# Three target tiles side by side instead of two in the attention stage of a two-layer graph kernel

## What is computed

```python
h = maximum(layernorm(x), 0)
x = x + max over neighbours of h            # layer 0, one row of adj per node
h = maximum(layernorm(x), 0)
g = h @ W                                   # layer 1: graph attention
e = (g @ a1)[:, None] + (g @ a2)[None, :]
e = where(e > 0, e, 0.2 * e)
att = softmax(where(adj > 0, e, -9e15), axis=1)
x = x + elu(att @ g)
```

## Time and profile before

| | |
|---|---|
| median of 3 runs | 797.32 us |
| profiled execution | 796.32 us, span 793.9 us |
| TensorE busy (matmul) | 708.5 us, 89% |
| VectorE busy | 722.7 us, 91% |
| ScalarE busy | 486.0 us, 61% |
| GpSimd busy | 283.4 us, 36% |
| mean granted TensorE clock | 0.985 |

### The profile page before, as it was taken

How to read it: one execution, slowest core, us unless ns; L and a number is a source line. 1 busy time by engine, 2 the same in 40 slices (tenths; PEclk the granted TensorE clock), 3 DMA queues, 4 the chain that set the end, 5 groups by cost and what they waited for, 6 DMA issues and landing times.

```text
span 793.9 us, 14766 instructions
## 1 busy us (share of the span) xinstructions
PE 708.5 (89%) x5592; PEld 484.5 (61%) x5592; DVE 722.7 (91%) x1120; ACT 486.0 (61%) x615; POOL 283.4 (36%) x258
## 2 busy tenths in 40 slices
PE   1788999999999999999999999788899999999995
PEld 1344444444444444444444444477789999999995
DVE  8899889999999999999999999999888998898894
ACT  2978888888888888888888888363523010010000
POOL 0612033443443443443443443453513432132130
PEclk9999999999999999999999999889999999999998
DMA  9699777997787777777777762723425444344410
GB/s 305 243 365 362 264 250 217 272 332 218 239 258 215 244 255 216 245 251 218 248 249 217 250 214 80 265 60 102 133 68 192 156 171 160 128 165 159 142 45 16
DMA packets 62856, 162.55 MB, mean 205 GB/s; under 512 B 6400, under 2 KB 11136, under 8 KB 58688
## 3 DMA queue, kind: packets, MB, share of 16 engines
q1 hardware_dynamic: 53776, 138.75, 50.8%
q0 software_dynamic: 9008, 22.82, 11.8%
HBM read 117.51 MB, written 44.04 MB: 203 GB/s over the span
## 4 chain that ended last, share of the span: by engine, by line
PE 40%; ACT 23%; DVE 18%; issue 11%; DMA 5%; POOL 1%; ACTq 0%; DVEq 0%; SPq 0%
PE pick_ps L667 21%; ACT edge_t L367 11%; PE pick_ps L570 7%; DVE acc L825 7%; PE order_ps L551 7%; ACT depth L376 7%; ACT first L375 4%; DVE rest L1004 4%; DMA found<-subset_max,entry 3%; PE late_ps L583 2%; DVE rest L814 2%; PE late_ps L542 2%; DMA subset_max<-keys 2%; POOL h_lo L310 1%; DMA best<-x 1%
## 5 line engine op out<-in xcount | busy, mean ns | idle before, releaser
L825 DVE TENSOR_TENSOR acc<-pick_ps,acc 128x1024 f32<-128x1024 f32 x248 | 303.0, 1222 | 28.2 <-PE pick_ps L570 23.7
L339 POOL DMA_INDIRECT found<-subset_max,entry x192 | 205.6, 1071 | 297.2 <-DVE entry L837 198.5
L667 PE MATMUL pick_ps<-keys,rest 128*128 128x129 f32 x2048 | 237.5, 277 | 6.8 <-DVE rest L1004 6.7
L667 PEld LDWEIGHTS pick_ps<-keys,rest 128*128 128x128 f32 x2048 | 233.7, 193 | 13.1 <-DVE rest L1004 11.4
L1004 DVE SCALAR_TENSOR_TENSOR rest<-depth,curves_sb,stage 128x512 f32<-128x512 f32 x256 | 200.7, 814 | 21.1 <-ACT curves_sb L455 5.2
L375 ACT ACTIVATE first<-order_ps,neg 128x1024 f16<-128x1024 f32 x128 | 142.6, 1114 | 61.2 <-PE order_ps L551 61.2
L376 ACT ACTIVATE depth<-order_ps,mid 128x1024 f16<-128x1024 f32 x128 | 141.7, 1107 | 0.0
L367 ACT ACTIVATE edge_t<-late_ps 128x1024 f16<-128x1024 uint16 x128 | 131.1, 1024 | 2.8 <-PE late_ps L542 2.8
L551 PE MATMUL order_ps<-edge_t,order_w 128*128 128x512 f16 x256 | 79.5, 393 | 38.2 <-ACT edge_t L367 30.8
L570 PE MATMUL pick_ps<-first,h_hi 128*128 128x512 f16 x256 | 98.1, 383 | 6.9 <-DVE acc L825 6.8
L542 PEld LDWEIGHTS late_ps<-ident_h,stage 128*128 128x128 f16 x1024 | 69.6, 100 | 49.2 <-DMA stage<-adj 13.2
(11 more groups left out here) (135 smaller groups left out, 517.9 us busy)
## 6 DMA issues: line engine op xcount, KB each, us to landing
stage<-adj SPq DMA_DIRECT2D x64, 1024.0 KB, 5.4
edge_units<-edge_t SPq DMA_DIRECT2D x64, 512.0 KB, 4.5
stage<-edge_units SPq DMA_DIRECT2D x32, 1024.0 KB, 5.1
subset_max<-keys POOLq DMA_DIRECT2D x12, 512.0 KB, 8.6
found<-subset_max,entry POOLq DMA_INDIRECT x192, 4.3
best<-x SPq DMA_DIRECT2D x4, 512.0 KB, 6.2
subset_max<-x POOLq DMA_DIRECT2D x4, 512.0 KB, 8.7
out<-keys POOLq DMA_DIRECT2D x7, 256.0 KB, 3.3
```

Source lines behind the costliest of these rows:

```text
L339: nc.gpsimd.indirect_dma_start(found[:, n % NG, s, :], None, subset_max, bass.IndirectOffsetOnAxis(entry[:, n, s:s + 1], 0)).then_inc(gath ...
L667: last = nc.tensor.matmul(out_ps(q, b), weight[:, n % WEIGHTS, b * P:(b + 1) * P], wh[:, c, :], start=c == 0 and b % 2 == 0, stop=c == C - ...
L825: V.tensor_tensor(acc[:, q % 2, :], pick_ps[k][:, :], acc[:, q % 2, :], ALU.max).then_inc(raised, 1)
```

## The change

Tiles 0, 1 and 2 now walk the source groups side by side (`TRIO = 3`), over groups 0 and 1, 2 and 3, 4 and 5, 6, and 7: products 0 to 95. Then come tiles 3 to 7. The twelve accumulators lie three to a bank in banks 0 to 2 and the fourth blocks of all three tiles in bank 3; tile 3 uses banks 6 and 7, later tiles banks 0 to 3 in pairs as before. `limit` has four slots. `bound(2)` moves into the part of groups 2 and 3, behind move(3) and ahead of curve(2). Side work on VectorE and TensorE has new product numbers. The sums of the three tiles are copied out together when product 95 is done. The core of the diff:

```diff
+        TRIO = 3
+        ORDER = [(q, c) for lo, hi in ((0, 2), (2, 4), (4, 6), (6, LAST), (LAST, GR)) for q in range(TRIO) for c in range(lo * ROWS, hi * ROWS)]
+        ORDER += [(q, c) for q in range(TRIO, TILES) for c in range(C)]
...
+        THIRD = 136
+        trio_ps = lambda q, b: banks[q][:, b * THIRD:b * THIRD + D + 1] if b < TRIO else banks[TRIO][:, q * THIRD:q * THIRD + D + 1]
+        pair_ps = lambda q, b: banks[(6 if q == TRIO else q % 2 * 2) + b // 2][:, b % 2 * APART:b % 2 * APART + D + 1]
...
+        row_ps = lambda g: banks[(4, 5, 0, 1, 5, 4, 5, 5)[g]]
+        col_ps = lambda g: banks[(6, 6, 4, 5, 4, 5, 4, 4)[g]]
+        source_ps = lambda q: banks[2 if q < 2 else 4 + q % 2]
...
# ScalarE
                     normalise(i)
                     move(PARTS[i][1] - 1)
+                    if i == 2:
+                        bound(2)
                     for g in range(*PARTS[i]):
                         curve(g)
                         gather_wh(g)
-                bound(2)
-                norm(0)
-                norm(1)
-                for q in range(2, TILES):
+                bound(TRIO)
+                for q in range(TRIO):
+                    norm(q)
+                for q in range(TRIO, TILES):
...
# TensorE, behind mix(n)
-                    if n in (8, 9):
-                        columns(n - 6)
-                    if n == 9:
-                        project(2)
-                    if n in (10, 11, 14):
-                        rows((10, 11, 14).index(n) + 4)
-                    if n == 11:
-                        project(3)
-                    if n in (25, 26, 29):
-                        columns((25, 26, 29).index(n) + 4)
-                    if n in (27, 30, 33):
-                        project((27, 30, 33).index(n) + 4)
-                    if n == 40:
-                        rows(LAST)
-                    if n == 52:
-                        columns(LAST)
-                    if n == 54:
-                        project(LAST)
-                    if n == 56:
-                        sources(2)
+                    if n in (10, 11):
+                        columns(n - 8)
+                    if n == 12:
+                        sources(2)
+                    if n in (12, 14):
+                        project(n // 2 - 4)
+                    if n in (18, 20, 27):
+                        rows((18, 20, 27).index(n) + 4)
+                    if n in (40, 42, 46):
+                        columns((40, 42, 46).index(n) + 4)
+                    if n in (42, 46, 50):
+                        project((42, 46, 50).index(n) + 4)
+                    if n == 52:
+                        rows(LAST)
+                    if n == 75:
+                        columns(LAST)
+                    if n == 77:
+                        project(LAST)
+                    if n == 82:
+                        sources(TRIO)
...
# VectorE, ahead of weigh(n): product numbers before -> after
# add(2), add(3)            1, 2   -> 2, 3      stat(2), stat(3)        3, 4   -> 4, 5
# moments(2)                5      -> 6         fold(7)                 6      -> 18
# scales(2)                 7      -> 8         join(26), join(27)      9, 17  -> 13, 21
# search(29), name(29)      10     -> 11        merge and add 4, 5      13, 14 -> 24, 27
# stat(4), stat(5)          15, 16 -> 28, 29    merge(6), add(6)        18     -> 31
# stat(6), moments(3)       19     -> 33        scales(3)               22     -> 36
# search(30), name(30)      24     -> 26        search(31), name(31)    28     -> 40
# join(28), join(29)        27, 30 -> 44, 48    over                    32     -> 52
# join(30)                  40     -> 56        join(31), merge, add 7  47     -> 67
# stat(7), moments(4)       48     -> 69        scales(4)               50     -> 72
+                    if n - WEIGHTS + 1 == ENDS[TRIO - 1]:
+                        for k in range(TRIO):
+                            sums(k)
+                        for k in range(TRIO):
+                            invert(k)
+                    if n - WEIGHTS + 1 in ENDS[TRIO:]:
+                        sums(ENDS.index(n - WEIGHTS + 1))
                         invert(ENDS.index(n - WEIGHTS + 1))
```

More of the change, by code:

```diff
@@ L180, in layers @@
         weight = rest.rearrange("p s w -> p (s w)").bitcast(F32).rearrange("p (s t) -> p s t", t=TI)
[L181 removed]
+        limit = depth[:, :, :].rearrange("p s w -> p (s w)").bitcast(F32).rearrange("p (s t) -> p s t", t=TI)
         wide = keys.rearrange("p h r w -> p (h r w)")
@@ L667, in mix @@
                         last = nc.tensor.matmul(out_ps(q, b), weight[:, n % WEIGHTS, b * P:(b + 1) * P], wh[:, c, :],
-                                                start=c == 0 and b % 2 == 0, stop=c == C - 1 and b % 2 == 1)
+                                                start=c == 0 and starts(q, b), stop=c == C - 1 and stops(q, b))
                     last.then_inc(mixed, 1)
@@ L993, in cap @@
                     dve.wait_ge(limited, q + 1)
-                    V.tensor_scalar(limit[:, q % 2, :], limit[:, q % 2, :], STEEP, None, ALU.min).then_inc(capped, 1)
+                    V.tensor_scalar(limit[:, q % 4, :], limit[:, q % 4, :], STEEP, None, ALU.min).then_inc(capped, 1)
                     dve.wait_ge(capped, q + 1)
@@ L1003, in weigh, with sums @@
                         dve.wait_ge(mixed, n - WEIGHTS + 1)
-                    V.scalar_tensor_tensor(out=weight[:, n % WEIGHTS, :], in0=limit[:, q % 2, :], scalar=slope[:, c:c + 1],
+                    V.scalar_tensor_tensor(out=weight[:, n % WEIGHTS, :], in0=limit[:, q % 4, :], scalar=slope[:, c:c + 1],
                                            in1=units[:, m % EDGES, k * TI:(k + 1) * TI], op0=ALU.max, op1=ALU.mult).then_inc(made, 1)
-                def invert(q):
-                    dve.wait_ge(mixed, ENDS[q] + 1)
+                def sums(q):
+                    dve.wait_ge(mixed, ENDS[max(q, TRIO - 1)] + 1)
                     for b in range(ROWS):
@@ L1035, in _ @@
                         cap(q)
[L1036 to L1040, removed]
+                    if n in (2, 3):
+                        add(n)
+                    if n in (4, 5):
+                        stat(n - 2)
+                    if n == 6:
                         moments(2)
-                    if n == 6:
-                        fold(TILES - 1)
-                    if n == 7:
+                    if n == 8:
@@ L1045, in _ @@
                         scales(2)
-                    if n == 9:
-                        join(C - 6)
-                    if n == 10:
+                    if n == 11:
                         search(C - 3)
                         name(C - 3)
[L1051 to L1056, removed]
-                        join(C - 5)
@@ L1058, in _ @@
-                    if n == 18:
+                    if n == 13:
+                        join(C - 6)
+                    if n == 18:
+                        fold(TILES - 1)
+                    if n == 21:
+                        join(C - 5)
+                    if n in (24, 27):
+                        merge(n // 3 - 4)
+                        add(n // 3 - 4)
+                    if n == 26:
+                        search(C - 2)
+                        name(C - 2)
+                    if n in (28, 29):
+                        stat(n - 24)
@@ L1059, in _ @@
+                    if n == 31:
                         merge(6)
                         add(6)
-                    if n == 19:
+                    if n == 33:
                         stat(6)
                         moments(3)
-                    if n == 22:
+                    if n == 36:
                         scales(3)
[L1066 to L1070, removed]
@@ L1071, in _ @@
-                    if n == 28:
+                    if n == 40:
                         search(C - 1)
                         name(C - 1)
-                    if n == 30:
+                    if n == 44:
+                        join(C - 4)
+                    if n == 48:
                         join(C - 3)
-                    if n == 32:
+                    if n == 52:
                         dve.wait_ge(entry_ready, C)
```

49 lines of the change are left out of this document (25 added, 24 removed).

## The result

The changed kernel takes 794.02 us (median of 5 runs, 792.97 to 795.24) against 797.94 for the kernel before in the same rounds: ratio 0.9957, 95% interval 0.9938 to 0.9976. Measured again in other rounds it was 794.49 us, ratio 0.9965 (0.9951 to 0.9979). The forecast was 794.2 us. So it is faster, by about 0.4%. The profiled execution took 794.1 us with a span of 792.1; before it was 796.32 and 793.9.

What follows compares the result with a forecast made beforehand. TensorE was taken as the bound from about 617 us; before that 13.7 us were lost, all the change could win. 796.32 - 5.6 + 0.8 + 2.5 = 794.0, with 0.2 carried over 794.2 us; range 791.0 to 797.4.

Steps and rivals of the forecast that it cites:

- Products 2 to 23, loss 0.1: Early products: VectorE keeps ahead of TensorE; ScalarE's chain before project(3) costs 0.1 us, ends 0 and 1.3.
- Products 24 to 40, loss 3.6 + 0.5: Crowded VectorE side work makes TensorE lose 3.6 us in products 24 to 37, and search(31) at product 40 another 0.5.
- columns(6) to project(5): After product 46: ScalarE's chain takes 4.30 us between their starts, and TensorE stands 3.9 us, none of it hidden.
- Products 53 to 95, loss 0: VectorE's lead covers the last side work and no load is late: no loss, ends 0 and 1.
- Won by product 95: 5.6: Start to product 95: 8.1 us still lost against 13.7 before, so 5.6 us won.
- Tile 3: 0.8 more than now: After product 95: three GpSimd closings in a row slow the weighs, 0.8 us more than now, ends 0 and 3.7.
- The clock: 2.5: Granted clock falls to 0.50 at the 3.9 us wait before project(5), costing 2.5 us, ends 0 and 3.5.
- Rest: 0: Three accumulators in a bank and four limit slots cost 0, ends -0.1 and +0.5 over 96 products.
- B: At the 3.9 us wait before project(5): clock does not fall, 791.7 us; chance 0.23.
- C: VectorE eats the gain: no lead at product 24 (+2.0), 1 to 2 us more in tile 3, 797; chance 0.19.
- D: Slower: clock falls three times, already in VectorE-bound products 26 to 37 and again at project(5), 802 us; chance 0.07.
- E: Waits lie elsewhere than on preparation; ScalarE delays what VectorE no longer does, 797.3 us; chance 0.06.

Runs made afterwards that it cites:

- experiment 1: Changed kernel with columns(6) after product 43 instead of 46, project(5) after 48 instead of 46, project(6) after 54: 788.99 us, ratio 0.9907 to the kernel before.
- experiments 3: Changed kernel with GpSimd's closings of tiles 1, 2 and 3 held 12 products apart: 793.54 us; again, 793.20 us, ratio 0.9962.
- experiment 4: Changed kernel with GpSimd's two tensor_tensor steps in the closings of tiles 0 to 2 cut to one column in 128: 792.82 us, ratio 0.9947.
- experiment 5: Changed kernel's three tiles side by side, but nearly all side work at the product numbers of the kernel before: 798.53 us, ratio 1.0028.
- experiment 2: Changed kernel with four idle matmuls filling the wait between columns(6) and project(5): 792.51 us, ratio 0.9952; again, 793.35 us.

## Why the prediction was right, step by step

- *Products 2 to 23, loss 0.1.* Product 24 starts at 549.99 + 3 x 0.893 = 552.7; the forecast had 552.9. But the way there is not the forecast's. The low clock of 521 to 528 us in the old trace is missing in the new one, and product 2 starts at 525.77 instead of 528.70. Counted from there 2.9 us are lost by product 24, more than the 2 us that the prediction named as a sign of being wrong. TensorE came early and waited for weights; the longest such wait stands ahead of product 8, and the second profile, with product 2 at 526.93, names its cause:

```profile
533.53 1.72 PE L678 MATMUL pick_ps<-keys,rest 128*128 128x129 f32 x13 [0.97 <-DVE rest L1015]
```

  The second profile of experiment 1, whose kernel is the same up to product 43, has the low clock and product 2 at 530.10. There product 24 starts at 551.70 + 3 x 0.893 = 554.4, 24.3 us later for 24.0 us of work: 0.2 lost, as the forecast had it. Counted from weigh 0 on VectorE, product 24 comes after 30.9 us in both profiles of the changed kernel and 31.3 in this one. So VectorE sets the pace here, and the low clock is worth about 0.4 us.
- *Products 24 to 40, loss 3.6 + 0.5.* From 552.7 to product 40 at 571.78 are 19.1 us for 16 products and one rows(), 14.7 us of work: 4.4 lost against 4.1. Waits for weights were not confined to products 26 to 37, as the signs of being right had it: short ones also stand ahead of products 5, 6, 8 and 40, and one in tile 3.
- *columns(6) to project(5).* 584.21 - 579.91 = 4.30 us, the forecast to the hundredth, idle 3.70. It is a chain of fixed steps on one other engine, released by the very instruction in front of the wait, and such a wait can be read from the old trace exactly. Experiment 1 shows that it is paid in full.
- *Products 53 to 95, loss 0.* There are small gaps, 0.23 us before product 72 the largest; in all some 0.5.
- *Won by product 95: 5.6.* Product 96 starts at 634.63; before it is 617.21 + 23 x 28.99/32 = 638.05. That is 3.4 us sooner, and with the clock's 1.6 added back 5.1. The term was too large by 0.5, about the small gaps just named.
- *Tile 3: 0.8 more than now.* Measured 1.5 against the old 0.4, that is 1.1 more. Most of the old 0.4 lies ahead of product 96, though, inside the term above: from product 96 to 137 it is 39.85 us against 38.45, 1.4 more. The mechanism is shown by experiments 3 and 4.
- *The clock: 2.5.* In the profiled execution 1.6. The term was sized after a spell of 7 us. Three of the five traces with this wait have such a spell and lose 2.6; the two with a spell of about 3.4 us lose 1.6.
- *Rest: 0.* In an undisturbed stretch with three accumulators in a bank, products 83 to 95 take (634.63 - 623.02)/13 = 0.893 us each, as before.
- *The sum.* The terms are off by 0.5, 0.6 and 0.9, and these errors cancel, which is luck: 796.32 - 5.1 + 1.4 + 1.6 = 794.2, and the profiled execution has 794.1. Luck has a part in the median too. The forecast was a fall of 3.1 us from 797.32; measured were 3.9 in the same rounds (797.94 to 794.02) and 2.3 in the others (796.77 to 794.49). In the four later groups of rounds the median of the kernel before lay between 796.42 and 796.77, below the 797.32 from which the forecast started. Whether a clock that falls at the old wait makes this scatter, as the prediction thought possible, is not shown: there is one trace of the kernel before.
- *The rivals.* B (no fall) did not come up in any of five traces. Of C the extra loss in tile 3 came, 1.1 to 1.4 us, but not its lead of zero at product 24. D did not occur: the crowded stretch 557 to 572 has a clock of 1.00 throughout. E is refuted by experiment 5: with the preparation left dense the waits on it come back and the gain is gone.

## What to carry to other kernels

When preparation work is spread over more of a main loop, place it by the chain that each step hangs on, and not only by load: two steps on the bound engine between which another engine has a chain of known length need products of that length between them, and here leaving them side by side gave away about 5 of the 10 us that the wider loop could win. Before a wait is covered, ask what is late next: the same edit won 5 us where the last gathers had room and lost 2 us where they had none. A change that lets three pieces end at once also bunches their closing work, and a queue of such work on a neighbour engine may need to be spaced by hand; here the trace shows 1.5 us for it and the time does not settle how much of that arrives.

## What the runs showed of the hardware

- A wait of 2.80 us left the granted clock at 1.00 in one kernel and was followed by a fall in another (experiment 5), each in one execution. 3.70 us were followed by a fall in five traces of five; a wait of 0.26 us behind 3.6 us of idle matmuls was not, in either trace of experiment 2. The price in the trace was 1.6 or 2.6 us, with the same kernel giving both in two executions. Matmuls that compute nothing, in a place where the engine stands anyway, kept the clock at 1.00 here.
- The low clock in front of product 2 comes and goes between executions of the same kernel: product 2 starts at 525.77 and 526.93 in the changed kernel, at 527.96 and 530.10 in that of experiment 1. In the last of these layer 1 began 1.4 us later than in the first, which is part of the distance.
- A weigh of 0.75 us takes 1.75 beside GpSimd's tensor_tensor of 1.6 us, and it can be read in the instruction count of a stretch of VectorE: 15 against 19 in 17 us (experiment 4).
